# A PE step takes one of the three banks longest free, by what it asks for, and waits that another wait implies are left out

## The reference

```
x = x + Nystrom(layernorm(x))      q, k, v = x Wqkv + b;  64 landmarks: means of 8 tokens
        attn1 = softmax(q k_l), attn2 = softmax(q_l k_l), attn3 = softmax(q_l k)
        V = attn2;  6 times:  KV = attn2 V;  V = 0.25 V (13 I - KV (15 I - KV (7 I - KV)))
        out = attn1 (V (attn3 v)) Wout + bout
x = x + CrossAttention(layernorm(x), ctx, mask)      64 keys for each batch element
x = x + FFN(layernorm(x))          x + 0.3 (gelu(x W1[e]) W2[e] Wo ...), expert e by the argmax of
                                   a gate on the last token of each batch element
```

## Time and profile before

| what | value |
|---|---|
| median of 3 runs | 1399.54 us (1398.2 to 1399.92) |
| the profiled execution | 1397.8 us, its span 1396.1 us |
| granted clock of TensorE | 0.998 |
| PE busy | 1355.2 us, 97% |
| VectorE busy | 1029.5 us, 74% |
| ScalarE busy | 667.0 us, 48% |
| GpSimd busy | 571.1 us, 41% |

### The profile page before, as it was taken

How to read it: one execution, slowest core, us unless ns; L and a number is a source line. 1 busy time by engine, 2 the same in 40 slices (tenths; PEclk the granted TensorE clock), 3 DMA queues, 4 the chain that set the end, 5 groups by cost and what they waited for, 6 DMA issues and landing times.

```text
span 1396.1 us, 53472 instructions
## 1 busy us (share of the span) xinstructions
PE 1355.2 (97%) x23732; PEld 889.7 (64%) x23732; DVE 1029.5 (74%) x2194; ACT 667.0 (48%) x1230; POOL 571.1 (41%) x799
## 2 busy tenths in 40 slices
PE   6998999999999999999999999999999999999998
PEld 4756666666766767665666766666666656676555
DVE  3487887758786886878778686877868777898641
ACT  2424355454555546355554644555454544435652
POOL 6223444443626244362534436153353543417132
PEclk9999999999999999999999999999999999999999
DMA  8002010120201011020101101010110100001122
GB/s 285 1 3 95 3 63 3 45 75 3 66 5 51 20 38 33 3 66 5 51 20 37 34 3 58 13 51 20 37 34 3 52 2 19 18 4 39 25 77 65
DMA packets 40536, 53.18 MB, mean 38 GB/s; under 512 B 9698, under 2 KB 30450, under 8 KB 40306
## 3 DMA queue, kind: packets, MB, share of 16 engines
q1 hardware_dynamic: 31602, 41.37, 9.2%
q10 hardware_dynamic: 8704, 8.39, 1.8%
HBM read 37.16 MB, written 12.59 MB: 36 GB/s over the span
## 4 chain that ended last, share of the span: by engine, by line
PE 85%; DVE 5%; ACT 3%; issue 2%; POOL 1%; DMA 1%; DVEq 1%; POOLq 0%; SPq 0%; ACTq 0%
PE bank L1322 41%; PE bank L1575 8%; PE bank L1341 7%; PE bank L1331 7%; PE bank L1564 3%; PE bank L1530 2%; PE bank L1418 2%; PE bank L1397 2%; PE bank L1462 2%; PE bank L1543 2%; PE bank L1451 2%; ACT p3T L896 1%; PE bank L1385 1%; PE bank L1562 1%; PE bank L1424 1%
## 5 line engine op out<-in xcount | busy, mean ns | idle before, releaser
L778 POOL TENSOR_TENSOR b<-ut,eye 128x256 f32<-128x256 f32 x192 | 137.6, 733 | 498.6 <-DVE ut L1161 428.9
L940 ACT ACTIVATE az<-bank 128x320 f32<-128x320 f32 x192 | 67.5, 400 | 185.6 <-PE bank L1331 185.2
L1322 PE MATMUL bank<-xnT_a,wqkv 128*128 128x512 f32 x256 | 123.6, 609 | 0.3 <-ACT xnT_a L864 0.3
L1218 DVE RECIPROCAL oT_x<-bank 128x256 f32<-128x256 f32 x64 | 109.2, 1733 | 19.2 <-PE bank L1575 19.2
L1322 PE MATMUL bank<-w2e,hT 128*128 128x256 f32 x512 | 119.0, 386 | 1.5 <-ACT hT L1006 1.4
L1218 DVE RECIPROCAL oT<-bank 128x256 f32<-128x256 f32 x64 | 111.5, 1747 | 10.6 <-PE bank L1575 10.6
L1322 PE MATMUL bank<-xnT_c,w1e 128*128 128x512 f32 x256 | 117.0, 597 | 1.3 <-DVE m_x L1192 0.9
L1090 DVE TENSOR_REDUCE m<-bank 128x1 f32<-128x512 f32 x128 | 82.9, 680 | 38.5 <-PE bank L1418 36.9
L1322 PEld LDWEIGHTS bank<-w2e,hT 128*128 128x128 f32 x512 | 96.0, 192 | 16.9 <-issue 2.7
L896 ACT ACTIVATE p3T<-bank 128x512 f32<-128x512 f32 x128 | 66.7, 603 | 79.1 <-PE bank L1451 78.9
L959 ACT ACTIVATE pT_x<-bank,neg_bias 128x512 f32<-128x512 f32 x128 | 79.9, 696 | 29.8 <-PE bank L1564 28.8
(11 more groups left out here) (223 smaller groups left out, 2979.2 us busy)
## 6 DMA issues: line engine op xcount, KB each, us to landing
x_in<-in_x SPq DMA_DIRECT2D x16, 512.0 KB, 3.8
w1e<-in_W SPq DMA_DIRECT2D x16, 512.0 KB, 3.5
w2e<-w2o SPq DMA_DIRECT2D x16, 512.0 KB, 4.1
out<-base ACTq DMA_DIRECT2D x32, 256.0 KB, 2.1
row_e<-w2o_row SPq DMA_DIRECT2D x16, 128.0 KB, 4.6
hT<-in_W2T SPq DMA_DIRECT2D x2, 512.0 KB, 6.5
pT_x<-in_ctxT SPq DMA_DIRECT2D x1, 1024.0 KB
ctxT<-in_ctxT SPq DMA_DIRECT2D x16, 64.0 KB, 2.6
```

The source lines that it names most:

```text
L778: return g.tensor_tensor(b7[:, q, :], ut[:, q, :], eye[28 if it else 7][:].unsqueeze(1) .broadcast_to([P, 4, LM]), ALU.subtract).then_inc( ...
L1218: return v.reciprocal(oT[x][:, k, cols], tile(i, ("den" + x, k))[:, cols]).then_inc(dve_done, 1)
L1322: last = mm(dst, lhsT, rhs, start=(k == 0), stop=(k == len(pairs) - 1))
```

## The change

plan() keeps, for PE, the highest count of A and of D that it has waited for (`waited`). A new function, operands(), names the operands of each PE step on A and D. For each bank of a step the first three of the list are priced: 0 if the bank's emptier is within what PE has waited for, 1 if it is beyond that and its engine is one for which this step waits already, 2 otherwise. The first of the cheapest is taken.

In the emission, due() and OPERANDS_FROM are gone. counts() collects what a PE step needs from A, D and G, for operands and banks together. It leaves out what PE has waited for, and also what another of the step's waits implies: `reached` holds, for each step of each engine, what that engine had itself waited for when it issued the step. What remains is waited for in an order that is written out for each kind. A wait that is issued also raises PE's record by all that it implies. The steps of A, D, G and S and their waits stay as they are.

```
--- before.py
+++ after.py
...
+def operands(step):
+
+    kind, n = step[0], step[1] if len(step) > 1 else 0
+    if kind in ("q", "k", "v"):
+        return [("A", ("xnTa", 0)), ("A", ("xnTa", 1))]
+    if kind in ("xnTb", "xnTc"):
+        return [] if step == ("xnTb", 0) else [("A", ("nmB",) if kind == "xnTb" else ("nmC", n))]
+    if kind in ("s3", "s1", "sx"):
+        return [("A", ({"s3": "k", "s1": "q", "sx": "qx"}[kind], n))]
+    if kind in ("t1", "tx"):
+        return [("A", ("mT" + kind[1],))]
+    if kind in ("x2T", "mT3", "t3", "mT1", "mTx"):
+        return [("D", ({"x2T": "soft2", "mT3": "mp3", "t3": "mT3", "mT1": "mp1", "mTx": "mpx"}[kind],))]
+    if kind in ("zT", "den1", "denx", "o1", "ox"):
+        e = {"z": "e3", "d": "e" + kind[-1], "o": "e" + kind[-1]}[kind[0]]
+        return [("A", (e, n, j)) for j in range(4)]
+    if kind in ("z", "a", "qx", "gate", "logit", "h", "y3"):
+        names = {"z": [("zT", 0), ("zT", 1)], "a": [("x2T",)], "qx": [("xnTb", 0), ("xnTb", 1)], "gate": [("xnTc", 1)],
+                 "logit": [("gate",)], "h": [("xnTc", 0), ("xnTc", 1)], "y3": [("h", f) for f in range(4)]}[kind]
+        return [("A", name) for name in names]
+    if kind in ("iT", "iZ"):
+        if n == 0:
+            return [("A", ("a", 0)), ("A", ("a", 1))]
+        return [("D", (x, n - 1, h)) for x in (("uz",) if kind == "iT" else ("uz", "ut")) for h in range(2)]
+    if kind in ("jT", "jZ"):
+        return [(e, (x, n, h)) for e, x in (("D", "wb"), ("A", "az")) for h in range(2)]
+    if kind == "y":
+        return [("D", ("uz", ITERS - 1, 0)), ("D", ("uz", ITERS - 1, 1))]
+    if kind in ("w1", "wx"):
+        return [("D", ("o" + kind[1], 0)), ("D", ("o" + kind[1], 1))]
+    return []
+
+
...
 def plan():
 
     done, count = {}, {}
     bank, before = {}, {}
     free = [(b, None) for b in range(BANKS)]
+    waited = {"A": 0, "D": 0}
     for engine, i, step in PROGRAM:
         if step[0] != "out":
             count[engine] = done[engine, i, step] = count.get(engine, 0) + 1
         if engine == "P":
+            asked = set()
+            for who, name in operands(step):
+                if done[who, i, name] > waited[who]:
+                    waited[who] = done[who, i, name]
+                    asked.add(who)
             for j in range(banks_of(step)):
-                bank[i, step, j], before[i, step, j] = free.pop(0)
+                price = [0 if emptier is None or done[emptier] <= waited[emptier[0]] else
+                         1 if emptier[0] in asked else 2 for _, emptier in free[:3]]
+                bank[i, step, j], emptier = free.pop(price.index(min(price)))
+                before[i, step, j] = emptier
+                if emptier and done[emptier] > waited[emptier[0]]:
+                    waited[emptier[0]] = done[emptier]
+                    asked.add(emptier[0])
...
-        passed = {}
+        passed, reached = {}, {}
 
         def first(eng, sem_, n):
 
-            if passed.get((eng, sem_), 0) >= n:
+            mine = passed.setdefault(eng, {})
+            if mine.get(sem_, 0) >= n:
                 return False
-            passed[eng, sem_] = n
+            mine[sem_] = n
             return True
...
-        def due(eng, who, emptied, i, *steps):
-
-            n = max(emptied[who], *[DONE[who, i, s] for s in steps])
-            return n if first(eng, done[who], n) else 0
+        def counts(eng, emptied, i, **steps):
+
+            need = {"A": emptied["A"], "D": emptied["D"], "G": 0}
+            for who, names in steps.items():
+                need[who] = max([need[who], *[DONE[who, i, s] for s in names]])
+            mine = passed.setdefault(eng, {})
+            need = {who: n for who, n in need.items() if n > mine.get(done[who], 0)}
+            left = {who: n for who, n in need.items()
+                    if not any(reached[other, m].get(done[who], 0) >= n for other, m in need.items())}
+            for who, n in left.items():
+                for sem_, m in (*reached[who, n].items(), (done[who], n)):
+                    mine[sem_] = max(mine.get(sem_, 0), m)
+            return {who: left.get(who, 0) for who in need.keys() | set("ADG")}
...
-        def run(who, body):
+        def run(who, eng, body):
             for engine, i, step in PROGRAM:
                 if engine == who:
                     body(i, step)
+                    if (who, i, step) in DONE:
+                        reached[who, DONE[who, i, step]] = dict(passed.get(eng, {}))
 
         def half(n):
...
-            run("G", body)
+            run("G", pool, body)
...
-                if "D" not in OPERANDS_FROM.get(kind, ""):
-                    if first(pe, dve_done, emptied["D"]):
-                        pe.wait_ge(dve_done, emptied["D"])
-                if "A" not in OPERANDS_FROM.get(kind, ""):
-                    if first(pe, act_done, emptied["A"]):
-                        pe.wait_ge(act_done, emptied["A"])
                 o = tile(i, step)
                 if kind == "kx":
...
                 elif kind in ("q", "k"):
-                    if c := due(pe, "A", emptied, i, ("xnTa", 0), ("xnTa", 1)):
-                        pe.wait_ge(act_done, c)
+                    c = counts(pe, emptied, i, A=[("xnTa", 0), ("xnTa", 1)])
+                    if c["D"]:
+                        pe.wait_ge(dve_done, c["D"])
+                    if c["A"]:
+                        pe.wait_ge(act_done, c["A"])
...
+                        c = counts(pe, emptied, i, G=[("b7", it, 0), ("b7", it, 1)],
+                                   **({"D": [("uz", it - 1, 0), ("uz", it - 1, 1)]} if it else {"A": [("a", 0), ("a", 1)]}))
+                        if c["A"]:
+                            pe.wait_ge(act_done, c["A"])
+                        if c["D"]:
+                            pe.wait_ge(dve_done, c["D"])
+                        if c["G"]:
+                            pe.wait_ge(pool_done, c["G"])
                         last = spread_out(i, step, uz, b7, LM, 0, LM)
                     else:
+                        c = counts(pe, emptied, i, D=[(x, it - 1, h) for x in ("uz", "ut") for h in range(2)] if it else [("z",)],
+                                   A=[] if it else [("a", 0), ("a", 1)])
+                        if c["A"]:
+                            pe.wait_ge(act_done, c["A"])
+                        if c["D"]:
+                            pe.wait_ge(dve_done, c["D"])
                         last = spread_out(i, step, ut, uz, LM + DH, 0 if it < ITERS - 1 else LM, LM + DH)
...
                 elif kind in ("jT", "jZ"):
                     it = n
-                    if c := due(pe, "D", emptied, i, ("wb", it, 0), ("wb", it, 1)):
-                        pe.wait_ge(dve_done, c)
-                    if c := due(pe, "A", emptied, i, ("az", it, 0), ("az", it, 1)):
-                        pe.wait_ge(act_done, c)
+                    c = counts(pe, emptied, i, A=[("az", it, 0), ("az", it, 1)], D=[("wb", it, 0), ("wb", it, 1)])
+                    if c["D"]:
+                        pe.wait_ge(dve_done, c["D"])
+                    if c["A"]:
+                        pe.wait_ge(act_done, c["A"])
...
```

More of the change, by code:

```diff
@@ L305, in emptied_by @@
     return None
-OPERANDS_FROM = {"q": "A", "k": "A", "v": "A", "s3": "A", "x2T": "D", "mT3": "D", "t3": "AD", "zT": "AD", "z": "A",
[3 rows of a table removed]
 FUSED = EXPERTS + 1
@@ L1013, in body @@
                     return last.then_inc(act_done, 1)
-            run("A", body)
+            run("A", act, body)
         @block.vector
@@ L1309, in body @@
                                                   ALU.mult, ALU.add).then_inc(dve_done, 1)
-            run("D", body)
+            run("D", dve, body)
         @block.tensor
@@ L1420, in body @@
                 elif kind == "s2":
-                    if c := unmet(pe, "G", i, ("qbd",), ("ksq",)):
-                        pe.wait_ge(pool_done, c)
+                    c = counts(pe, emptied, i, G=[("qbd",), ("ksq",)])
+                    if c["A"]:
+                        pe.wait_ge(act_done, c["A"])
+                    if c["D"]:
+                        pe.wait_ge(dve_done, c["D"])
+                    if c["G"]:
+                        pe.wait_ge(pool_done, c["G"])
                     for k in range(KD):
@@ L1431, in body @@
                 elif kind == "mT3":
-                    if c := due(pe, "D", emptied, i, ("mp3",)):
-                        pe.wait_ge(dve_done, c)
+                    c = counts(pe, emptied, i, D=[("mp3",)])
+                    if c["A"]:
+                        pe.wait_ge(act_done, c["A"])
+                    if c["D"]:
+                        pe.wait_ge(dve_done, c["D"])
                     for k in range(KD):
@@ L1453, in body @@
                 elif kind == "zT":
-                    if c := due(pe, "D", emptied, i, ("v", 0), ("v", 1)):
-                        pe.wait_ge(dve_done, c)
```

(52 more changed lines are left out.)

173 lines of the change are left out of this document (104 added, 69 removed), and 3 rows, old and new, of the table OPERANDS_FROM.

## The result

The changed kernel takes 1417.97 us (median of 4 runs, 1416.55 to 1418.29) where the kernel before takes 1399.49 (4 runs beside it). The ratio is 1.0131, 95% interval 1.0115 to 1.0146: 18.5 us slower by the medians, 18.3 by the ratio. Forecast were 8.1. The direction was right and the size was less than half of what came.

What follows compares the result with a forecast made beforehand. PE, busy 97% of the span, was taken to bound the kernel. Repeating steps 4.8 + single places 4.1 - stalls removed 0.3 - waits 0.5 = +8.1 us, giving 1407.6 us as a median, range 1398 to 1418.

Steps and rivals of the forecast that it cites:

- PE bounds it, and a later PE step lengthens it: Whole kernel: PE is busy 97% of the span, so a later PE step lengthens it unless PE would soon stand still.
- A satisfied wait costs 0: PE step boundaries: an already satisfied wait costs 0, at most its 51 ns, as the sequencer is ahead of the array.
- Waits left out, -0.5: PE steps with separate waits: fewer waits bring 0.5 us, between 0 and an upper end of 4.4.
- Bank stalls removed, -0.3: jT.0 of turn 1 saves 0.15 us, two more 0.13 together; the 2.33 us before vt stay.
- Gross prices of the picks named: Added bank stalls: t1.1 6.2 us, a 2.4, s1.1 1.0, 17 single places 8.2; gross 17.8 us.
- Each choice was judged on the free list of before: Stated limit: passed-over banks can heal or spoil later choices; unhealed, unabsorbed end +17.8 us, healed end about 0.
- rivals 2 and 3: No change, healed by later lists: 1399.5 to 1402, chance 0.24; passed-over banks pushing further steps to young banks: 1417, chance 0.10.
- Snowball: Passed-over banks push further steps to young banks and the half absorbed is not: +17.8, 1417 us, chance 0.10.
- jT.2 absorbs 2.5, t1.1 costs 3.7: Turns 3 to 12: jT.2, standing still for wb anyway, absorbs 2.5 of t1.1's 6.2 us, so t1.1 costs 3.7.
- of 2.4 us 0.6 stays. Of s1.1 I leave 0.5: xnTb.1 behind a waits for xn_b anyway, so 0.6 of a's 2.4 us stays; s1.1 keeps 0.5 of 1.0.
- The same half on 8.2 is 4.1: 17 single places in first and last turns: half of 8.2 us stays, 4.1, as repeating steps keep 4.8 of 9.6.

Runs made afterwards that it cites:

- e4: Kernel before with two more long-satisfied waits ahead of the first matmul of each of the 1291 PE steps: 1400.04 us, ratio 1.0009.
- e1: Changed kernel, but every PE step takes the longest free bank again, so only the new waits are left: 1397.56 us, ratio 0.9987.
- e11: Changed kernel with longest-free-first at iT.1 alone: 1412.49 us, ratio 1.0102 to the kernel before.
- e7: Kernel before, but in turns 3 to 12 t1.1 takes the second free bank instead of the first for its last bank: 1402.30 us, ratio 1.0025.
- e9: Changed kernel with its new price at t1.1, a and s1.1 alone, longest free bank elsewhere: 1406.49 us, ratio 1.0057 to the kernel before.
- e6: Changed kernel with longest-free-first at t1.1, a, s1.1 and iT.1: 1404.28 us, ratio 1.0046 to the kernel before.
- e3: Changed kernel without the middle price, so a raised count on an engine already asked costs as much as any other: 1396.36 us, ratio 0.9973.
- e10: e3 with the wait that ends last put first at five kinds of repeating steps: 1396.26 us, ratio 0.9982 to the kernel before.

## Why the prediction was right and wrong

- *PE bounds it, and a later PE step lengthens it*: right. The steady turn grew by 1.08 us, of which the seven boundaries named above hold 1.15.
- *A satisfied wait costs 0*: right, by e4. *Waits left out, -0.5*: it was -1.8 (e1), inside the bound of 4.4. Of it 0.8 comes from the two waits on ScalarE at xnTb.1 that became one, which I had not priced.
- *Bank stalls removed, -0.3*: right as far as it goes. jT.0 of turn 1 is 0.15 earlier, and vt's 2.2 us stay.
- *Gross prices of the picks named*: right nearly to the hundredth. t1.1 +0.62 forecast and +0.63 measured, a +0.21 and +0.20, s1.1 +0.11 and +0.11. Of the five single places priced by name, t3.1 of turn 1 +1.1 and +1.12, t3.0 of turn 3 +1.0 and +1.04, t1.1 of turn 13 +0.8 and +0.85, xnTb.1 of turn 1 +0.8 and +0.80, s3.1 of turn 14 +0.9 and +0.62.
- *"Each choice was judged on the free list of before"*: **this step failed.** On the changed kernel's own plan, against the same releases of before, the gross is 26.2 us in some 60 steps, not 17.8. The largest that it missed is iT.1, 0.39 in each of ten turns, worth 4.1 us by e11. Others are xnTc.0 of turn 14 (+1.3 in the trace of after), tx.0 of turn 0 (+1.2) and tx.1 of turn 12 (+1.0). It was not the list alone: the prices also go by what PE has waited for, and a replay gives the forecast's gross (17.9 for 17.8) only if that record too is the one of before. With the lists of before but the record as the new picks leave it, the replay has all ten stalls of iT.1 and some 4 of the 8 us missed. The prediction called this step the least trusted, and gave rivals 2 and 3 to it. "Snowball", with 0.10, is what came by its mechanism. That its +17.8 us is also near the 18.3 is luck: it is the gross of the old lists with nothing absorbed, where a gross of 26.2 came with some 6 absorbed.
- *"jT.2 absorbs 2.5, t1.1 costs 3.7"*: the 2.5 are right (2.6 in e7), the 3.7 are not. den1.1 stood without slack on a ScalarE chain that starts at t1.1, and takes back 1.7. Of ten turns of t1.1, 5.0 stays.
- *"of 2.4 us 0.6 stays. Of s1.1 I leave 0.5"*: both too small. By e9 against e1, a keeps 1.5, since half of the 0.18 that xnTb.1 was to give back had already gone with its second wait (e1). s1.1 keeps all; its half had no row behind it.
- *"The same half on 8.2 is 4.1"*: wrong. The first and last turns cost 8.3 us (e6 over e1). In the trace of after, boundaries there that differ by over 0.1 us gain 14.6 and give back 5.9. The half was carried over from three steps, of which two have a stall of their own close behind (jT.2, xnTb.1), and all three kept more than thought.

By the ratios the miss comes apart so. The steps t1.1, a and s1.1 take 9.8 us (e9 over e1, three of their single places in turns 1, 13 and 15 with them) where 4.8 + 0.8 were forecast, iT.1 4.1 where nothing was, the other places in the first and last turns 8.3 (e6 over e1) where 3.3 was, the waits -1.8 where -0.5 was, and the stalls removed -0.3 are in these numbers. That is 20.4 against 18.3 measured, each term known to some 2 to 3 us. In one line of kernels, where each is built on the last, it closes: -1.8 (e1), +8.3 (e6 over e1), +11.9 (changed over e6), 18.4.

Open: why the steps behind the single places gave back so little, and whether e3's picks are worth anything beyond e1. A kernel without the new price at t1.0 and ox.0 was not run, nor windows other than three banks.

## What to carry to other kernels

When a rule changes who gets which buffer, replay the whole allocation with the new rule before pricing it against measured release times: one changed pick alters later lists and the record of what has been waited for, and here the picks seen on the old ones were two thirds of the stall. A satisfied wait cost nothing measurable here, and a younger buffer cost most of its lateness, so a count should not be raised to save a wait unless the buffer is known to be free by then. Before a delay is called absorbed by the next stall, follow what the delayed step feeds: a chain without slack returns it a few steps later.

## What the hardware showed that was not expected

- The wait issued first rides on the weight load, and the matmul starts 43 to 47 ns behind its release (xnTb.1 in e1, tx.1 in e10). One that is in a separate instruction takes 135 ns (t3.1, jT.0, tx.1 and xnTb.1 before, to within 1 ns where nothing else binds). Which of two waits is first is thus worth up to 0.09 us where it ends last: all of it at tx.1, 50 to 65 ns at jT.0 and t3.1.
- With two satisfied conditions added (e4) the same boundaries take 90 ns and not 135. The trace does not say why.
- A separate wait instruction can hold two conditions, and 1291 more of them, 51 ns each by their own duration, moved the kernel by 1.3 us.
